# WKV layers 1 to 3: the backward scan runs over the forward scan's result, the terms are scaled on ScalarE first, and two idle products stand ahead of the first expert group's rows

## The reference

```python
def _bi_wkv(r, k, v, w, u, time_emb):          # r = x, k = v = fside
    tf = jax.nn.sigmoid(jnp.sum(time_emb, axis=-1))[:, None, None]
    decay = jnp.exp(-jnp.exp(w))[None, :] * (0.5 + 0.5 * tf[:, :, 0])
    ek = jnp.exp(jnp.minimum(k, 30.0))
    ekv = ek * v
    def step(carry, x):
        a, b = carry
        ekv_t, ek_t = x
        a = a * decay + ekv_t
        b = b * decay + ek_t
        return ((a, b), (a, b))
    _, (nf, df) = lax.scan(step, init, (ekv_t, ek_t))
    _, (nb, db) = lax.scan(step, init, (ekv_t, ek_t), reverse=True)
    euk = jnp.exp(jnp.minimum(u + k, 30.0))
    num = nf + nb - ekv + euk * v
    den = df + db - ek + euk
    return jax.nn.sigmoid(r) * (num / jnp.maximum(den, 1e-08)) * (0.8 + 0.2 * tf)
...
x = x + _L0_ffn_ref(_L0_cond_ref(x, ...), ...)
x = x + _L1_ffn_ref(_L1_cond_ref(x, ...), ...)
x = x + _L2_ffn_ref(_L2_cond_ref(x, ...), ...)
x = x + _L3_ffn_ref(_L3_cond_ref(x, ...), ...)
```

## Time and profile before

| quantity | value |
|---|---|
| median of 3 runs | 503.69 us (502.92 to 503.91) |
| the profiled execution's own time | 505.18 us |
| span of the profiled execution | 503.2 us |
| PE busy | 431.2 us, 86% of the span |
| DVE busy | 380.1 us, 76% |
| ACT busy | 195.3 us, 39% |
| POOL busy | 102.9 us, 20% |
| mean granted clock of PE | 0.925 of full |

### The profile page before, as it was taken

How to read it: one execution, slowest core, us unless ns; L and a number is a source line. 1 busy time by engine, 2 the same in 40 slices (tenths; PEclk the granted TensorE clock), 3 DMA queues, 4 the chain that set the end, 5 groups by cost and what they waited for, 6 DMA issues and landing times.

```text
span 503.2 us, 5667 instructions
## 1 busy us (share of the span) xinstructions
PE 431.2 (86%) x2007; PEld 269.0 (53%) x2010; DVE 380.1 (76%) x681; ACT 195.3 (39%) x339; POOL 102.9 (20%) x63
## 2 busy tenths in 40 slices
PE   0696999987971389999999999999999999998583
PEld 0241564676761157999899898743444444433130
DVE  3989898797799897867677678547666745738995
ACT  4450255471122368223343773334011004135880
POOL 0000000000000088511200000005757555551000
PEclk9998678989976599999999999979999999999798
DMA  7920000540077024767534552602000000000001
GB/s 285 407 87 1 1 0 0 208 160 1 0 220 239 21 53 104 241 216 227 155 107 156 189 193 91 266 1 86 0 0 1 1 0 0 0 0 2 0 33 50
DMA packets 12108, 47.86 MB, mean 95 GB/s; under 512 B 2881, under 2 KB 5290, under 8 KB 9650
## 3 DMA queue, kind: packets, MB, share of 16 engines
q1 hardware_dynamic: 10930, 43.58, 24.5%
q0 software_dynamic: 1152, 3.93, 3.2%
HBM read 45.14 MB, written 2.37 MB: 94 GB/s over the span
## 4 chain that ended last, share of the span: by engine, by line
PE 69%; DVE 21%; DMA 3%; issue 2%; ACT 2%; SPq 1%; POOL 0%; POOLq 0%; DVEq 0%
PE bank L1471 9%; PE bank L1445 9%; PE bank L1560 7%; PE bank L1573 7%; PE bank L1480 5%; PE bank L1605 4%; PE bank L1602 4%; PE bank L1334 3%; DMA wrb<-in_w_router 3%; PE bank L1376 2%; PE bank L1366 1%; PE bank L1536 1%; DVE arena L924 1%; PE bank L1295 1%; PE bank L1437 1%
## 5 line engine op out<-in xcount | busy, mean ns | idle before, releaser
L1445 PE MATMUL bank<-onehot,rows 128*128 128x512 f32 x192 | 51.4, 406 | 0.0
L353 POOL DMA_INDIRECT arena<-token_rows,arena x24 | 34.2, 1425 | 70.2 <-DVE arena L942 35.5
L595 ACT ACTIVATE early<-bank 128x512 f32<-128x512 f32 (+1 forms) x24 | 14.3, 597 | 84.2 <-PE bank L1573 75.8
L1471 PEld LDWEIGHTS bank<-arena 128*96 128x96 f32 x512 | 44.2, 165 | 3.9 <-issue 3.8
L1471 PE MATMUL bank<-arena 128*96 128x48 f32 x512 | 44.8, 248 | 0.2
L1156 DVE TENSOR_TENSOR early<-early,bank 128x512 f32<-128x512 f32 (+1 forms) x24 | 16.4, 685 | 37.5 <-ACT early L595 24.1
L364 POOL TENSOR_TENSOR early<-early,arena 128x512 f32<-128x512 f32 (+1 forms) x12 | 21.6, 1803 | 104.3 <-DMA arena<-pair_weights 99.6
L1573 PE MATMUL bank<-arena 128*128 128x512 f32 (+1 forms) x96 | 42.2, 600 | 0.2
L1560 PE MATMUL bank<-cT,arena 128*128 128x512 f32 x80 | 39.8, 623 | 0.0
L1445 PEld LDWEIGHTS bank<-onehot,rows 128*128 128x128 f32 x192 | 33.9, 189 | 6.1 <-DVE onehot L973 0.3
L1480 PEld LDWEIGHTS bank<-arena 96*128 96x128 f32 x256 | 30.7, 192 | 2.5 <-issue 0.7
(11 more groups left out here) (320 smaller groups left out, 881.7 us busy)
## 6 DMA issues: line engine op xcount, KB each, us to landing
arena<-in_w_gate SPq DMA_DIRECT2D x8, 768.0 KB, 5.1
arena<-in_w_up SPq DMA_DIRECT2D x8, 768.0 KB, 8.1
arena<-in_w_down SPq DMA_DIRECT2D x8, 768.0 KB, 9.9
const<-in_const SPq DMA_DIRECT2D x1, 2122.5 KB, 12.3
arena<-in_wq SPq DMA_DIRECT2D x1, 2048.0 KB
arena<-in_wo SPq DMA_DIRECT2D x1, 2048.0 KB, 8.2
arena<-in_w_upgate SPq DMA_DIRECT2D x1, 1408.0 KB, 5.8
kT<-in_kT SPq DMA_DIRECT2D x2, 512.0 KB, 5.3
```

The costliest lines, as they stand in the source:

```text
L353: g.indirect_dma_start(xg[:, t % XRING, :], None, scratch[:, :], bass.IndirectOffsetOnAxis(ap=toki[:, t:t + 1].bitcast(U32), axis=0)).then ...
L1445: return mm(bank[2 * ct + ch][:], rows1[:, i % RRING, part, ct * P:(ct + 1) * P], onehot1[:, t, ch * CHUNK:(ch + 1) * CHUNK], start=False, ...
L1471: last = mm(bank[bk][0:F1, e * CAP:(e + 1) * CAP], w[:, e, ct * F1:(ct + 1) * F1], xgT[g % 2][:, ct, e * CAP:(e + 1) * CAP], start=(ct == ...
```

## The change

Writing d for the decay, the two-sided sum with the token itself counted once is what a backward scan over the forward scan's result gives, up to a factor: if F is the forward scan of x, then z(t) = F(t) + d z(t+1) with z(T) = F(T-1) d/(1 - d^2) equals the two-sided sum divided by (1 - d^2). The changed kernel multiplies the terms by `gain` = (1 + d)(1 - d), at least 2^-40, ahead of the scans, so that nothing is left to do after them.

- ACT, new `scaled(l, kind)`: eight Copy activations of 128 x 256 with a per-partition scale (one for each half and batch), from `ekT` or `ekvT` into the layer's own buffer. There are six calls, 48 activations. They stand: (1,0) and (1,1) behind layer 0's guess; (2,0) behind `euk(1)`, ahead of the onehotT copies; (2,1) behind `gate(1)`; (3,0) behind `euk(2)`, ahead of the first `rows_in` copies; (3,1) in group 3.
- DVE, `forth` and `back_again` take the place of the pairs of scans: four forward scans in place, a product of 128 x 4 that makes the start values `ends`, then four backward scans in place that start from them. `forth` waits with `step` for its last scan and for the product. The twelve sums L657 and L668 go, and the three `last_tokens` of layers 1 to 3.
- The buffers rotate: den is in wB, wC, wA and num in wA, wB, wC for layers 1, 2, 3. `euk(l)` for l of 2 or 3 now waits for `num` of the layer before, not for a sum.
- DVE makes `gain` and `reach` = d/gain once, in five small operations on 128 x 6 x 4, behind layer 0's first eight scans.
- `euk(1)` moves ahead of the two onehotT copies on ACT.
- PE: `idle(6, 2)`, two products of 512 columns, ahead of `rows_in(0)`.

```diff
+            def scaled(l, kind):
+                for ct in range(CT):
+                    if l == 1:
+                        act.wait_ge(S("gain_ready"), 1)
+                        act.wait_ge(S("num0_done"), 2 * ct + 2)
+                    elif (l, kind) == (2, 0):
+                        act.wait_ge(S("c0_ready"), B)
+                    else:
+                        act.wait_ge(S("ratio_ready"), l - 2 + kind if l == 3 else 1)
+                    for b in range(B):
+                        bb = slice(b * T, (b + 1) * T)
+                        last = s.activation((den_buf, num_buf)[kind][l][:, ct, bb], (ekT, ekvT)[kind][:, ct, bb], ACT.Copy,
+                                            scale=gain[:, 2 * l - 2 + ct, b:b + 1])
+                    last.then_inc(S("scaled"), 1)
...
             guess_exp(0)
+            scaled(1, 0)
+            scaled(1, 1)
...
             euk(2)
+            scaled(3, 0)
...
+            def forth(l, kind, ct):
+                buf = (den_buf, num_buf)[kind][l]
+                dve.wait_ge(S("scaled"), 2 * CT * (l - 1) + CT * kind + ct + 1)
+                for b in range(B):
+                    x = buf[:, ct, b * T:(b + 1) * T]
+                    last = v.tensor_tensor_scan(x, dec[:, 2 * l + ct, b:b + 1].to_broadcast([P, T]), x, 0.0, ALU.mult, ALU.add)
+                step(last)
+                step(v.tensor_tensor(ends[:, kind, ct, :], buf[:, ct, T - 1::T], reach[:, 2 * l - 2 + ct, :], ALU.mult))
+
+            def back_again(l, kind, ct):
+                buf = (den_buf, num_buf)[kind][l]
+                for b in range(B):
+                    x = back(buf, ct, b, 0, T)
+                    v.tensor_tensor_scan(x, dec[:, 2 * l + ct, b:b + 1].to_broadcast([P, T]), x, ends[:, kind, ct, b:b + 1],
+                                         ALU.mult, ALU.add).then_inc(S(("den_scans", "num_scans")[kind]), 1)
...
             for ct in range(CT):
                 dve.wait_ge(S("ek_ready"), ct + 1)
                 for b in range(B):
-                    den_scans(0, ct, b)
+                    den_scans(ct, b)
+                if ct == 0:
+                    d = dec[:, CT:, :]
+                    step(v.tensor_scalar(reach[:], d, -1.0, 1.0, ALU.mult, ALU.add))
+                    step(v.scalar_tensor_tensor(gain[:], d, 1.0, reach[:], ALU.add, ALU.mult))
+                    step(v.tensor_scalar(gain[:], gain[:], GAIN_MIN, None, ALU.max))
+                    v.engine_nop().then_inc(S("gain_ready"), 1)
+                    step(v.reciprocal(reach[:], gain[:]))
+                    step(v.tensor_tensor(reach[:], reach[:], d, ALU.mult))
...
             for b in range(B):
                 v.tensor_scalar(onehot[:, b * T:(b + 1) * T], bank[5][:, 0:T], jrank, ofbatch[:, b:b + 1],
                                 ALU.is_equal, ALU.mult).then_inc(S("onehot_ready"), 1)
-            for b in range(B):
-                den_scans(1, 1, b)
-            den_sum(1, 0)
-            den_sum(1, 1)
-            num_scans(1, 0, 0)
-            num_scans(1, 0, 1)
+            back_again(1, 0, 0)
+            forth(1, 0, 1)
+            back_again(1, 0, 1)
...
             cond(1)
-            last_tokens(wD)
-            for b in range(B):
-                den_scans(2, 0, b)
-            den_sum(2, 0)
-            den_scans(2, 1, 0)
+            forth(2, 0, 0)
+            back_again(2, 0, 0)
+            forth(2, 0, 1)
             dve.wait_ge(S("small1_in"), 80)
             dve.wait_ge(S("score1"), 1)
...
-            for b in range(1, B):
-                den_scans(2, 1, b)
+            back_again(2, 0, 1)
             shared_product(0)
-            den_sum(2, 1)
             shared_product(1)
             den(2, 0)
             den(2, 1)
-            for b in range(B):
-                num_scans(2, 0, b)
-            num_scans(2, 1, 0)
+            forth(2, 1, 0)
+            back_again(2, 1, 0)
+            forth(2, 1, 1)
...
+            idle(6, 2)
             rows_in(0)
             shared_down(1, 0)
```

More of the change, by code:

```diff
@@ L85 @@
 DEN_MIN = 1e-8
+GAIN_MIN = 2.0 ** -40
 def build(nc, I, out):
@@ L110, in build @@
         dec = sb("dec", [P, 2 * LAYERS, B])
-        AC, A2 = 20660, 5120
+        gain, reach = (sb(n, [P, 2 * (LAYERS - 1), B]) for n in ("gain", "reach"))
+        ends = sb("ends", [P, 2, CT, B])
+        AC, A2 = 20640, 5120
         arena = sb("arena", [P, AC])
@@ L465, in _ @@
                 s.copy(ctok0[:, 2 * j:2 * j + 2, :], bank[1 + j][:].rearrange("p (a c) -> p a c", a=2)).then_inc(S("ctok0_ready"), 1)
+            euk(1)
+            scaled(2, 0)
             for j in range(2):
@@ L808, in _ @@
                 dve.wait_ge(S("qk_ready"), j + 1)
-            num_scans(1, 0, 2)
-            num_scans(1, 0, 3)
-            num_scans(1, 1, 0)
+            forth(1, 1, 0)
+            back_again(1, 1, 0)
             def att_peak(j):
@@ L831, in _ @@
             att_share(3)
-            for b in range(1, B):
-                num_scans(1, 1, b)
-            num_sum(1, 0)
-            num_sum(1, 1)
+            forth(1, 1, 1)
+            back_again(1, 1, 1)
             num_own(1, 0)
```

100 lines of the change are left out of this document (39 added, 61 removed).

## The result

The changed kernel takes 507.8 us (median of 4 runs, 507.07 to 511.11) beside 503.8 us for the kernel before (4 runs, 502.92 to 504.15): ratio 1.0087, 95% interval 1.0064 to 1.011. It is 0.9% slower. The profiled execution took 507.42 us, with a span of 505.6. The profiled one of the kernel before took 505.18, longer than its runs, so the two profiles lie 2.4 us apart in span where the medians lie 4.0 apart: what follows explains those 2.4, and the rest is scatter between executions that no profile shows.

A forecast was written before the change was run, and what follows sets the result against it. PE was busy 86% of the span and DVE 76%; WKV work could be on the path only ahead of the group loop. 0 - 0.13 + 0.52 + 1.03 = +1.42 us moved 503.69 to 505.1 us, range 503.6 to 506.3.

The forecast's parts named there:

- Start of the program: Ahead of layer 0's Newton step: DVE's five added small operations, 1.1 us, disappear in its wait for ACT; 0.
- Picking stage: 47 to 75 us: PE's bias and gathering products end late, so most of DVE's saving becomes waiting; -0.13 us.
- Rival 2: Picking stage: with PE at 2.4 GHz DVE's saving counts, -3.2 us instead of -0.13, time 502.0 us; chance 0.10.
- Layer 0: 75 to 143 us: scan pairs get shorter inside DVE's waits and nobody waits for them; no change.
- Condition: Behind layer 1's condition: DVE's longer scan sequence delays L881 and the expert choice from 7.10 to 7.62 us; +0.52.
- Ahead of gate_up(0): ACT's eight scaled(3, 0) activations, 0.38 us each, hold the first group's row copies and PE; +1.03 us.
- rival 3: Ahead of gate_up(0): idle products meet PE at 1.2 GHz, some 5 us later than now, 509; chance 0.06.
- Idle products: Ahead of rows_in(0): two products, 1.7 us, fit into PE's wait for the rows by under 0.1 us; 0.
- Group loop: From group 0 on: existing waits absorb the moved work and the loop passes the shift on unchanged; 0.
- Behind the loop: After the last group: no change expected; 0.

The follow-up runs named there:

- e6: Kernel before plus idle products in four of PE's waits and the change's two ahead of rows_in(0); 504.22 us, ratio 1.0006.
- e7: Changed kernel plus the same idle products in PE's waits as e6, so the two differ by the WKV edits alone; 499.58 us, ratio 0.9928.
- after: The changed kernel's first profile, against the kernel before; profiled execution 507.42 us, median 507.8 us, ratio 1.0087.
- e8: The changed kernel run once more, unchanged, on the chip of e5, e6 and e7; median 513.73 us, no ratio given.
- e2: Changed kernel without the two idle products ahead of rows_in(0); 512.16 us, ratio 1.0116.
- e3: Changed kernel with scaled(3, 0) moved into group 1 and without the two idle products ahead of rows_in(0); 513.99 us, ratio 1.0137.
- e5: e7 with scaled(3, 0) moved into group 1, forth(2, 0, 1) behind the expert choice and forth(2, 1, 1) into group 0; 500.62 us, ratio 0.991.
- e9: Changed kernel with only e7's two early idle groups, after the second batch's picking product and ahead of the router logits' wait; 508.24 us, ratio 1.0087.
- e11: e5 plus idle products in layer 0, ahead of the first two attention transposes and the second normalisation's transposes; 497.2 us, ratio 0.9864.
- e1: Changed kernel with scaled(3, 0) moved on ACT from behind euk(2) into group 1; 509.7 us, ratio 0.9996.
- e10: Changed kernel with only e7's two late idle groups, ahead of the waits for the routing weights and the expert table; 505.68 us, ratio 0.9998.
- e4: Kernel before plus only the two idle products ahead of rows_in(0); 507.09 us, ratio 1.0035.

## Why the prediction was wrong

Term by term; the comparison of e6 with e7 is the change with the clock held up.

- **Start of the program, 0.** The picking product starts 0.51 us earlier after, 0.25 earlier in e7 than in e6. But in two profiles of the same kernel, after and e8, it starts at 46.75 and 48.20 us, so this can't be told from 0. Right, within that.
- **Picking stage, -0.13: wrong.** It was -3.82 after, and -3.22 with the clock held up. The step that failed is "PE is in the bias products L1295 from 53.50 to 58.31, and L1302 stands behind them". That row is true of the execution that was profiled, in which the granted clock was 0.50 from 46 to 52 us and again from 56. In eight of the ten profiles made from the changed kernel the products end before DVE is ready, and DVE's saving counts. In after it is 1.61 us up to the rank product and 1.43 from the onehots to the gathered rows (7.82 instead of 9.25); the other 0.8 are PE's small products at the faster clock. The forecast had the second saving at 1.9: it is less because a backward scan takes 0.65, not 0.58. Rival 2 described this mechanism with a price of -3.2 and got a chance of 0.10, on the argument that the change moves nothing on PE ahead of 56 us; that e6 and e7 give just its sum, out of -2.00 and -1.22, is luck. The rank product comes 9.1 to 9.5 us behind the picking product in after, e2, e3, e5, e7, e8, e9 and e11, 10.85 in e1 and e10, 11.1 in the three profiles of the kernel before and its variants. The code ahead of this place is the same in after, e1, e2, e3, e8 and e10, and four of them have the short distance. So the argument was beside the point: the clock there is not a property of the code alone. That the kernel before can have it without keepers too was not seen.
- **Layer 0, 0.** -0.63 after, -0.99 with the clock held up. It can't be told from 0: the same kernel took 67.53 us in after and 68.16 in e8, and e2, with the same code there, 65.71.
- **Condition, +0.52.** L920 comes 7.90 us after the first scan instead of 7.10: +0.80. The mechanism is right. The sizes missed by a little each: four forward scans and their tail take 2.46 us, not 2.42; and four backward ones, whose start value is read from SBUF, take 2.60, 0.65 each instead of the 0.58 taken. The range for such scans (up to 0.2 more each) had it.
- **Ahead of gate_up(0), +1.03.** From the silu to gate_up(0) it is 8.12 instead of 7.07 us, +1.05, in after and in e7. Right. An activation took 0.40 us where I took 0.38. The Trainium skill ("ScalarE: Activation LUTs", section "What ACT_TABLE_LOAD costs") gave 0.40, and this trace agrees. What the forecast did not have is the +2.38 of the slow shared expert in after, ahead of the silu. It is akin to rival 3, with half its price and in another place: the clock was nearly back when L1439 began (0.84 from 176 to 178 us), but the second L1424 had run at 1.2 GHz. The forecast had taken the clock of one execution here too.
- **Idle products, 0.** Right for the changed kernel. e7, e8 and e10 show them hidden, with rows that come 0.28 to 0.32 us after them. In after they don't fit ahead of the rows, because PE is late by the slow shared expert, but ACT's activations hide them: without them (e2) the stage takes 46.00 us, with them 46.12. Where the shared expert was slow and no activations hold the copies, they stand on PE's path with their 1.72 us (e1 and e4, both 44.67).
- **Group loop, 0: wrong, and the largest miss.** Groups 1 to 7 do pass the shift on (-0.13). Group 0 does not: +4.91 us, 21.33 against 16.42. The step that failed is "the loop passes the shift on as it is", together with "PE's granted clock is already 1.00 (2.4 GHz) in this gap, so the products have nothing to give back in this execution": no term and no rival had the clock fall again. I counted ACT's hold of 1.03 us as a wait with its own length as the price. In the runs a wait of PE of 0.75 to 2.48 us in or just ahead of the first group, behind a routing stretch in which PE is nearly idle, came with a clock of 1.2 GHz for the next stretch, at 4.9 to 5.2 us (12.1 in e3), in all six profiles that had both and were made from the changed kernel (after, e1, e2, e3, e8, e9). With the quiet stretch filled (e7, e10) a wait of 0.94 to 0.96 us cost its own length. That filling the stretch keeps the clock is well supported, by two profiles and by the ratios of e9 and e10; that the wait sets off the fall is only likely: e4 has the stretch and almost no wait and no fall, but the kernel before has the stretch and a wait of 1.79 us and no fall in its profile either. What tells that one from e3 stays open.
- **Behind the loop, 0.** -1.65 after, and -1.59 in e7 against e6. I took nothing for it. It is 180.48 to 185.72 us in the profiles made from the changed kernel, so a difference of 1.6 shows little; what of it is the WKV work and what the clock was not separated.

So the sum of the terms with the clock held up is -0.25 - 3.22 - 0.99 + 1.87 - 0.01 - 0.11 - 1.59 = -4.3 us by the spans of e6 and e7; after's own is +2.4, as its clock takes away 4.9 in group 0 and 2.4 ahead of it. The forecast got the sign right, by luck, from a sum in which large terms of opposite sign were missing: -3.7 in the picking stage, +2.4 by the slow shared expert and +4.9 in group 0.

## What to carry to other kernels

When a stage's working rests on PE being the late engine, look at its granted clock there; if it is at 1.2 GHz behind a quiet stretch, work out the sum for both levels and give both a real chance, because the level may differ between executions of the same kernel. A new wait of 1 us of PE shortly behind a quiet stretch may be priced by what follows at half clock, not by its own length. An edit whose gain vanishes is worth a second try with the clock held up in both kernels, by idle products in PE's waits: here the same change is 0.9% slower without and 0.7% faster than the kernel before with them.

## What the hardware showed that was not expected

- The fall needs more than the wait itself. PE waited 0.99 us in e8 and 0.94 in e10 at the same place with the granted clock at 1.00, and only e8's fell, some microseconds later. What differs in the code is 8.2 us of idle products at 160 and a few more at 171, long before.
- The same waits and the same rows ahead of them can keep the clock in one execution and lose it in another: the kernel before (1.79 us, clock at 1.00) and e3 (1.98 us, clock at 0.50 from 184 to 210).
- Long executions of a kernel are those with a low mean granted clock: e1 from 502.45 us at 0.943 to 512.35 at 0.909, e8 from 505.83 at 0.934 to 519.15 at 0.898. e11's four lie at 496.79 to 497.87 and 0.962 to 0.971. A low clock need not scatter: e9's four lie within 1.9 us at 0.932 to 0.937.
- Idle products bring nothing where they take away no fall that costs time (e6, ratio 1.0006), and 1.5% where they do: e7 against after, by their ratios 0.9928 and 1.0087.
- A scan of 256 elements whose start value is a column in SBUF takes 0.65 us from start to start, one with a constant start 0.58, forwards (L692 here) and backwards (L643 before).
